# Moving the 16 padding transfers of each FFN from SyncE's queue ahead of the expert tiles to between the loads of tiles 24 to 31, with another order of tiles

## The reference

```
scores = softmax(xt @ Wg.T)                       # 16 experts in 4 groups
# the best 2 groups by their best expert, then the best 4 experts inside them
h = silu(einsum('td,eid->eti', xt, W1)) * einsum('td,eid->eti', xt, W3)   # inner width 176
y = sum over the 4 chosen experts of (h @ W2[e].T) * score
z = silu(xt @ Ws1.T) * (xt @ Ws3.T) @ Ws2.T       # shared expert, inner width 352
x = x + y + z
```

## Time and profile before

| | |
|---|---|
| Three executions, median | 1353.41 us (1342.67 to 1368.69) |
| The profiled execution's own time | 1349.85 us, of which the span of the trace is 1348.1 us |
| TensorE matmuls busy | 1144.7 us, 85% of the span |
| VectorE, ScalarE, GpSimd busy | 873.5, 541.6, 689.1 us |
| Chain that ended last | TensorE 57%, VectorE 18%, issue 6%, DMA 6%, ScalarE 6%, GpSimd 2%, SyncE's queue 2% |
| DMA | 169.84 MB, mean 126 GB/s |
| Padding transfers | 32 issues, 66.2 KB each |

### The profile page before, as it was taken

The page is one execution under the profiler, slowest core; times in us unless marked ns, Lnnn a source line. Parts: engine busy times, 40 slices in busy tenths (PEclk is TensorE's granted clock), DMA queues, the critical chain, the costliest instruction groups (busy, mean ns, idle before and its releaser), DMA issues.

```text
span 1348.1 us, 26055 instructions
## 1 busy us (share of the span) xinstructions
PE 1144.7 (85%) x8706; PEld 614.0 (46%) x8706; DVE 873.5 (65%) x2067; ACT 541.6 (40%) x846; POOL 689.1 (51%) x841
## 2 busy tenths in 40 slices
PE   6888999998899699999288899999779859999990
PEld 2343444342655366566154344444246435665650
DVE  5688899981576145555388899999568523554543
ACT  2124777779431122222032577777844001222210
POOL 4452344544036577767552454545521652787671
PEclk9897999999889799999699899999988978999995
DMA  4424433320825479987754321221062345898868
GB/s 144 144 86 126 122 109 121 106 64 2 287 72 149 150 183 164 158 156 113 192 178 143 108 61 53 62 50 50 3 255 48 113 129 144 168 159 161 153 91 262
DMA packets 145875, 169.84 MB, mean 126 GB/s; under 512 B 20240, under 2 KB 130768, under 8 KB 145232
## 3 DMA queue, kind: packets, MB, share of 16 engines
q1 hardware_dynamic: 115856, 128.79, 32.7%
q0 software_dynamic: 29184, 38.36, 16.7%
q10 hardware_dynamic: 704, 1.02, 0.2%
HBM read 93.29 MB, written 76.18 MB: 126 GB/s over the span
## 4 chain that ended last, share of the span: by engine, by line
PE 57%; DVE 18%; issue 6%; DMA 6%; ACT 6%; POOL 2%; SPq 2%; another core or an unknown queue 1%; POOLq 0%; ACTq 0%; DVEq 0%
PE pair_ps L1996 11%; PE o_ps L1761 9%; ACT arena L849 4%; DVE nm L1123 4%; PE pair_ps L2029 4%; DMA x_slots<-y_sb,slot_i 3%; DVE bm L1123 3%; PE pair_ps L2032 2%; PE t_ps L1787 2%; PE pair_ps L1711 2%; PE pair_ps L1592 2%; PE pair_ps L1691 2%; PE pair_ps L1716 2%; PE pair_ps L2003 2%; PE pair_ps L1686 2%
## 5 line engine op out<-in xcount | busy, mean ns | idle before, releaser
L849 ACT ACTIVATE arena<-pair_ps 128x1024 f32<-128x1024 f32 x320 | 322.9, 1024 | 130.6 <-PE pair_ps L1686 75.9
L625 POOL TENSOR_SCALAR_AFFINE_SELECT arena<-arena 128x512 f32<-128x512 f32 (+1 forms) x320 | 175.0, 547 | 241.4 <-ACT arena L849 240.9
L1123 DVE TENSOR_REDUCE nm<-pair_ps 128x2 f32<-128x1024 f32 (+1 forms) x192 | 232.6, 1222 | 33.4 <-PE pair_ps L1735 29.5
L687 POOL DMA_INDIRECT x_slots<-y_sb,slot_i x128 | 123.6, 966 | 168.0 <-DVE slot_i L1321 94.0
L1761 PE MATMUL o_ps<-arena 128*9 128x512 f32 (+7 forms) x2048 | 176.8, 440 | 4.2 <-POOL arena L625 4.1
L1996 PE MATMUL pair_ps<-arena 128*128 x512 | 168.6, 471 | 2.5 <-ACT arena L900 2.5
L1123 DVE TENSOR_REDUCE bm<-pair_ps 128x8 f32<-128x1024 f32 x128 | 155.3, 1217 | 4.1 <-PE pair_ps L1735 1.0
L703 POOL DMA_INDIRECT y_h<-xnT,dest x80 | 125.3, 1567 | 58.6 <-DVE xnT L1480 31.4
L703 POOL DMA_INDIRECT y_f<-xnT,dest x80 | 124.6, 1558 | 42.0 <-issue 21.2
L1463 DVE TENSOR_TENSOR arena<-arena,pair_ps 128x128 f32<-128x128 f32 x144 | 41.4, 288 | 116.6 <-ACT arena L905 77.1
L1996 PEld LDWEIGHTS pair_ps<-arena 128*128 128x128 f32 x512 | 93.8, 195 | 43.9 <-issue 6.3
(11 more groups left out here) (275 smaller groups left out, 2012.8 us busy)
## 6 DMA issues: line engine op xcount, KB each, us to landing
arena<-x_slots SPq DMA_DIRECT2D x128, 132.5 KB
arena<-in_w SPq DMA_DIRECT2D x4, 2816.0 KB, 18.9
arena<-q_a SPq DMA_DIRECT2D x64, 96.0 KB
arena<-q_b SPq DMA_DIRECT2D x64, 96.0 KB
y_f<-hw SPq DMA_DIRECT2D x11, 512.0 KB, 2.9
y_h<-hw SPq DMA_DIRECT2D x11, 512.0 KB, 2.9
arena<-in_w SPq DMA_DIRECT2D x2, 2048.0 KB, 17.4
arena<-y_f SPq DMA_DIRECT2D x8, 512.0 KB
```

The lines of the kernel that those rows point to most:

```text
L625: pool.affine_select(p, p, pattern, ALU.is_ge, 0.0, base=0, channel_multiplier=-1)\
L687: pool.indirect_dma_start(x_slots, bass.IndirectOffsetOnAxis(ap=slot_i[:, t, k:k + 1], axis=0), y_sb[:, t, :], None).then_inc(sm(f"scat{n ...
L849: act.activation(p_ring[:, U % RING, :], pair_ps[:, pair_at("T", n, u)].rearrange("p a c -> p (a c)"), ACT.Exp, scale=SCALE).then_inc(sm(" ...
L1123: dve.tensor_reduce(dst, src, X, ALU.max, negate=not 2 <= u < 4).then_inc(sm("t_max_done"), 1)
```

## The change

The paddings are no longer issued first. SyncE's queue now starts with the wait for the order of tiles and the stores of x, and it issues two paddings behind each of the loads of tiles 24 to 31 (`PAD_FIRST`, `PADS`). The load of tile 32 waits until all 16 have landed (`PADDED`). For this no tile ahead of 32 may need padding: the tiles are ordered by levels. Level one, as before, are tiles full by the first 10 groups of tokens; level two are the other tiles that are full in the end; then come the rest. So there are two columns where there was one in `full`, in the counts and in the scan, and VectorE's ordering code is written for a list of levels. Mixed tiles stand at 35, 39, ..., 63 instead of 29, 35, ..., 71; the second weights of the first four are loaded at tiles 8, 16, 26 and 34 as before, those of the others at 47, 51, 55 and 59 instead of 41, 47, 53 and 59. The scatters keep their order and number: 52 ahead of the tiles, waits for 40 and for all 64 at the same tiles as before.

```diff
@@ -56,7 +56,7 @@
 NJ = 72
 PLAIN = 64
 MIXED = NJ - PLAIN
-MIX = tuple(range(29, NJ, 6))
+MIX = tuple(range(35, 64, 4))
 MR = 4
 MIX_AT = (8, 16, 26, 34) + tuple(j + 12 for j in MIX[:4])
 ROUND = 1.5 * 2 ** 23
@@ -72,14 +72,15 @@
 
 XR = 8
 WR = 6
-EARLY_T = 10
-EARLY = 24
-LATE_FIRST = 12
+LEVELS = (10, 16)
+NL = len(LEVELS)
+PAD_FIRST, PADS, PADDED = 24, 2, 32
+FIRST_X = 52
 
 assert (ROWS * TOPK + NE * (HALF - 1)) // HALF <= 2 * NJ <= 2 * P and NJ % XR == 0 and XR == 2 * B
 assert ROWS * TOPK // P <= PLAIN and NE <= 2 * MIXED and MIXED == len(MIX) <= XR
-assert all(j % 2 == 1 and j >= EARLY for j in MIX)
-assert EARLY * P <= EARLY_T * P * TOPK - NE * (P - 1)
+assert all(j % 2 == 1 and j >= TOPK * LEVELS[-2] - NE for j in MIX) and MIXED == len(range(MIX[0], MIX[-1] + 1, 4))
+assert PAD_FIRST + NE // PADS <= PADDED <= min(MIX[0], TOPK * NT - NE) and LEVELS[-1] == NT
 SCH = [(0, 128), (128, 128), (256, 96)]
 M_DMAS = 2 * 16
 
...
@@ -215,7 +216,13 @@
-        full = sb("full", [P, 1], BF16)
+        full = sb("full", [P, NL], BF16)
+        lev = sb("lev", [P, NL, NE])
+        lev_r = sb("lev_r", [P, NL])
+        lev_f = sb("lev_f", [P, NL + 2])
+        lev_d = sb("lev_d", [P, NL])
+        lev_v = sb("lev_v", [P, NL + 1])
+        lev_h = sb("lev_h", [P, NL + 1])
...
@@ -492,26 +499,29 @@
             def row_of(j):
                 return sp.value_load(first_row[0:1, j:j + 1], min_val=0, max_val=SLOT_ROWS - P)
 
-            sp.wait_ge(sm("e_pads"), 1 + past(f, 1))
-            for e in range(NE):
+            def padding(e):
                 row = sp.value_load(pad_row[0:1, e:e + 1], min_val=0, max_val=EMPTY - HALF)
                 sp.dma_start(x_slots[ds(row, HALF), :], x_slots[EMPTY:EMPTY + HALF, :]).then_inc(sm("padded"), 16)
+
             sp.wait_ge(sm("e_order"), 1 + past(f, 1))
             for b in range(B - 1):
                 store_x(b)
-            sp.wait_ge(sm("padded"), 16 * NE * (1 + past(f, 1)))
-            for parity in range(2):
-                sp.wait_ge(sm(f"scat{parity}"), 16 * (EARLY_T * TOPK // 2 + past(f, NT * TOPK // 2)))
             for j in range(NJ):
                 if j == 4:
                     store_x(B - 1)
                 if j >= XR:
                     sp.wait_ge(sm("e_x_tr"), j - XR + 1 + past(f, NJ))
                     sp.wait_ge(sm("e_dest"), (j - XR) // 4 + 1 + past(f, NJ // 4))
-                if j == EARLY:
-                    for parity in range(2):
-                        sp.wait_ge(sm(f"scat{parity}"), 16 * (NT * TOPK // 2) * (1 + past(f, 1)))
+                for t, first in zip(LEVELS, (0,) + tuple(TOPK * t - NE for t in LEVELS)):
+                    if j == first:
+                        for parity in range(2):
+                            sp.wait_ge(sm(f"scat{parity}"), 16 * (t * TOPK // 2 + past(f, NT * TOPK // 2)))
+                if j == PADDED:
+                    sp.wait_ge(sm("padded"), 16 * NE * (1 + past(f, 1)))
                 load(j)
+                for e in range(PADS * (j - PAD_FIRST), PADS * (j - PAD_FIRST + 1)):
+                    if 0 <= e < NE:
+                        padding(e)
                 if j in MIX_AT:
                     second_weights(MIX_AT.index(j))
                 if j % 2 == 1:
@@ -718,9 +728,9 @@
             for n in range(TH * TOPK):
                 scatter(n)
             pool.wait_ge(sm("e_slots"), 2 + past(f, 2))
-            for n in range(TH * TOPK, EARLY_T * TOPK + LATE_FIRST):
+            for n in range(TH * TOPK, FIRST_X):
                 scatter(n)
-            late = range(EARLY_T * TOPK + LATE_FIRST, NT * TOPK)
+            late = range(FIRST_X, NT * TOPK)
             for j in range(NJ):
                 result_out(j)
                 for n in late[2 * j:2 * j + 2]:
@@ -1327,10 +1337,10 @@
                 kpre, single, end, pairs, first, last = (tot[:, i, :] for i in range(6))
                 c = spare[:, 0:NE * NE].rearrange("p (i j) -> p i j", i=NE)
                 total = s_ps[:, 0, NT * NE:(NT + 1) * NE]
-                early = s_ps[:, 0, (NT + 1) * NE:(NT + 2) * NE]
+                early = s_ps[:, 0, (NT + 1) * NE:(NT + 1 + NL) * NE].rearrange("p (l e) -> p l e", l=NL)
                 dve.scalar_tensor_tensor(pad_row[:], experts_i, float(REGION), total, ALU.mult, ALU.add)\
                     .then_inc(sm("e_pads"), 1)
-                ch(dve.tensor_scalar(a[:, 0, :], early, 0.5 - HALF, 1.0 / P, ALU.add, ALU.mult))
+                ch(dve.tensor_scalar(lev[:], early, 0.5 - HALF, 1.0 / P, ALU.add, ALU.mult))
                 ch(dve.tensor_scalar(nt[:, 0, :], total, HALF / 2 - 0.5, 1.0 / HALF, ALU.add, ALU.mult))
                 rounded(nt[:, 0, :])
                 ch(dve.tensor_tensor(c, low16.rearrange("p (i j) -> p i j", i=NE),
@@ -1345,15 +1355,18 @@
                 ch(dve.scalar_tensor_tensor(first, kpre, -1.0, nt[:, 1, :], ALU.mult, ALU.add))
                 ch(dve.tensor_scalar(first, first, 0.5, None, ALU.mult))
                 ch(dve.tensor_tensor(last, first, pairs, ALU.add))
-                rounded(a[:, 0, :])
-                ch(dve.tensor_tensor(a[:, 1, :], a[:, 0, :], first, ALU.add))
+                rounded(lev[:])
+                ch(dve.tensor_tensor(lev[:], lev[:], first.unsqueeze(1).to_broadcast([P, NL, NE]), ALU.add))
                 ch(dve.tensor_scalar(a[:, 2, :], last, lane, None, ALU.is_le))
-                ch(dve.tensor_scalar(a[:, 3, :], a[:, 1, :], lane, None, ALU.is_le))
-                ch(dve.tensor_reduce(r[:, 0:2], a[:, 2:4, :], X, ALU.add))
+                ch(dve.tensor_scalar(lev[:], lev[:], lane, None, ALU.is_le))
+                ch(dve.tensor_reduce(r[:, 0:1], a[:, 2, :], X, ALU.add))
+                ch(dve.tensor_reduce(lev_r[:], lev[:], X, ALU.add))
                 ch(dve.tensor_scalar(r[:, 2:3], r[:, 0:1], float(NE - 1), -float(NE), ALU.min, ALU.add))
-                ch(dve.tensor_tensor(r[:, 3:4], r[:, 2:3], r[:, 1:2], ALU.subtract))
-                ch(dve.tensor_scalar(r[:, 3:4], r[:, 3:4], 1.0 + NE, None, ALU.add))
-                dve.tensor_copy(full[:], r[:, 3:4]).then_inc(sm("e_full"), 1)
+                ch(dve.tensor_scalar(r[:, 3:4], r[:, 2:3], 1.0 + NE, None, ALU.add))
+                ch(dve.memset(lev_f[:, 0:1], 1.0))
+                ch(dve.memset(lev_f[:, NL + 1:NL + 2], 0.0))
+                ch(dve.tensor_scalar(lev_f[:, 1:NL + 1], lev_r[:], -1.0, r[:, 3:4], ALU.mult, ALU.add))
+                dve.tensor_copy(full[:], lev_f[:, 1:NL + 1]).then_inc(sm("e_full"), 1)
 
             def pair_units():
 
@@ -1387,11 +1400,13 @@
 
                 r = ordc
                 dve.wait_ge(sm("e_scan"), 1 + past(f, 1))
-                ch(dve.tensor_copy(r[:, 4:5], s_ps[:, 1, 0:1]))
-                ch(dve.tensor_scalar(r[:, 5:6], r[:, 4:5], float(EARLY), lane_late, ALU.min, ALU.subtract))
-                ch(dve.tensor_scalar(r[:, 6:7], r[:, 4:5], float(EARLY), r[:, 3:4], ALU.is_lt, ALU.mult))
-                ch(dve.tensor_tensor(r[:, 7:8], r[:, 4:5], r[:, 5:6], ALU.add))
-                ch(dve.tensor_scalar(r[:, 7:8], r[:, 7:8], r[:, 6:7], r[:, 5:6], ALU.mult, ALU.subtract))
+                ch(dve.tensor_copy(lev_v[:, 0:1], lane))
+                ch(dve.tensor_copy(lev_v[:, 1:NL + 1], s_ps[:, 1, 0:NL]))
+                ch(dve.tensor_tensor(lev_d[:], s_ps[:, 1, NL:2 * NL], lev_v[:, 1:NL + 1], ALU.subtract))
+                ch(dve.tensor_tensor(lev_v[:, 0:NL], lev_v[:, 0:NL], lev_d[:], ALU.add))
+                ch(dve.tensor_tensor(lev_h[:], lev_f[:, 0:NL + 1], lev_f[:, 1:NL + 2], ALU.subtract))
+                ch(dve.tensor_tensor(lev_v[:], lev_v[:], lev_h[:], ALU.mult))
+                ch(dve.tensor_reduce(r[:, 7:8], lev_v[:], X, ALU.add))
                 ch(dve.tensor_tensor(r[:, 7:8], r[:, 7:8], own1[:, 7:8], ALU.add))
                 dve.tensor_scalar(place[:, 0, :], tiles_i, r[:, 7:8], own1[:, 6:7], ALU.is_equal, ALU.mult)\
                     .then_inc(sm("e_place"), 1)
...
@@ -1907,7 +1922,7 @@
                 last = NT if hf == 1 else TH - 1
                 for t in range(last):
                     first = max(t + 1, hf * TH)
-                    n = (TH if hf == 0 else NT + 1) - first + (1 if hf == 1 and t < EARLY_T else 0)
+                    n = (TH if hf == 0 else NT + 1) - first + (sum(t < first_t for first_t in LEVELS) if hf == 1 else 0)
                     mm = pe.matmul(s_ps[:, 0, first * NE:(first + n) * NE].rearrange("p (n e) -> p n e", n=n), ones,
                                    taken[:, t, :].unsqueeze(1).to_broadcast([P, n, NE]), start=False, stop=t == last - 1,
                                    skip_group_check=True)
@@ -1915,7 +1930,8 @@
 
             def scan():
                 pe.wait_ge(sm("e_full"), 1 + past(f, 1))
-                pe.matmul(s_ps[:, 1, 0:1], upper, full[:], start=True, stop=True, skip_group_check=True)\
+                pe.matmul(s_ps[:, 1, 0:NL], upper, full[:], start=True, stop=False, skip_group_check=True)
```

(17 more changed lines are left out.)

## The result

| | kernel before | changed kernel |
|---|---|---|
| device time, median | 1356.72 us of 4 | 1379.77 us of 4 (1378.88 to 1392.61) |
| execution with the trace, own time / span | 1349.85 / 1348.1 us | 1378.88 / 1377.1 us |
| ratio | | 1.023, 95% interval 1.012 to 1.034 |
| once more, on another chip, fast median | 1353.4 of 10 | 1384.0 of 4; ratio 1.020 (1.014 to 1.027) |

The account below looks back on a forecast made before the run. GpSimd's scatters bind the first FFN's opening; the loop looks bound by TensorE, but SyncE's queue hardly waits. Opening -15.2, mixed tiles -2.2, loop +34.6 sum to +17.2 on 1349.85: 1367 us, range 1332 to 1395.

Parts of the forecast that it names:

- the forecast's own range: Whole kernel: 1355 to 1380 us around the forecast, for slower issues or landings, uncovered ordering, start or lead; chance 0.42.
- Paddings into the loop: Expert loops: 16 issues of 1.19 us plus landing, less cover, delay later loads; 16.2 and 18.4 us, +34.6 together.
- landing wait: Load of tile 32 in the expert loop: waits for the last padding to land, 0.85 us per FFN.
- cover: Expert loop: loads' time in hand, 1.9 and 1.4 us, plus a 1.75 us queue pause in the first FFN.
- Paddings out of the opening: Start of each FFN: 0 gained in the first, 17.5 less 2.3 us in the second; -15.2 us.
- freeze: Second FFN's opening: no matmul or VectorE instruction from 1074 to 1085, ScalarE's silu late; taken to belong to the paddings.
- slower start: Second FFN's first tiles: a start following hard on the scatters is slower, giving back 2.3 us.
- the freeze is chance: Rival, opening: freeze comes in some executions with or without paddings, so the -15.2 falls away; 1382 us, chance 0.14.
- Ordering: Opening of each FFN: extra ordering operations, about 1 us, are covered; cost 0 in both.
- Mixed tiles: Tiles 35 to 63: last tile loses its second scatter, 1.85 us less, 0.72 back; -1.1 per FFN, -2.2.
- Hidden: Rival, expert loop: SyncE's queue has more room and the leads absorb 20 us; 1332 us, chance 0.22.
- The freeze moves: Rival, expert loop: paddings stay slow beside GpSimd's transfers, 2.58 us each; 1389 us, in both FFNs 1412; chance 0.22.

Follow-up runs that it names:

- quarter size: Changed kernel with its paddings back in the opening, plus 16 more of 16 rows instead of 64 behind loads of tiles 24 to 31: 1400.1 us, ratio 1.034.
- one per tile: Changed kernel with one padding behind each load of tiles 16 to 31 instead of two behind each of 24 to 31: 1374.9 us, ratio 1.012.
- row numbers read ahead: Changed kernel with the paddings' 16 row numbers read into registers ahead of the wait for the ordering: 1357.0 us, ratio 1.013.
- ScalarE's in both orders: Paddings issued by ScalarE, two behind each silu of chunks 4 to 11: changed kernel 1342.1 us, ratio 0.988; kernel before 1337.0 us, ratio 0.998.

## Why the prediction was right, and where it was not

**Forecast against result.** 1367 was forecast, 1378.9 measured on the execution with the trace: +17.2 against +29.0 (the medians are 23 apart). The mechanism was right, the loop term too small. From first to last transpose the loops are 26.8 and 27.2 us longer, not the 16 to 18 given as a sign of being right. The additions named for the forecast's own range reach 1376, not its stated 1380, so the end of the range held the result with nothing in the sum behind it: that part was luck. The other signs came: TensorE waits for loads at tiles 27, 31 and 35 in both FFNs, and load 32 waits under 1 us.

**Paddings into the loop, +34.6 predicted, +43.8 measured (22.6 and 21.2).** This is the mis-sized term. The landing wait was right (0.85, 0.9 measured) and so nearly was the issue: taken at 1.19 us, while 21.2 without the landing wait leaves 1.27. Some cover was there too. Counted from tile 24 and with the mixed tile allowed for, the load of tile 35, the last for which TensorE waits, is 20.9 and 19.1 us late and its transpose 18.8 and 18.5. So the cover was worth 2.1 and 0.6, where the sum had 3.65 and 1.4; the pause of 1.75 in it stood at load 40, too late to help. What the sum put at nothing is TensorE's time behind its last wait, the largest error: the transpose of tile 36, whose load is there in time, is 22.6 and 21.2 late.

```profile
561.72 0.69 PE L1987 MATMUL o_ps<-c_f,arena 128*128 128x128 f32 x2 [2.57 <-DMA arena<-x_slots]
563.05 0.90 PE L2019 MATMUL pair_ps<-c_f,arena 128*128 128x128 f32 x3 [0.64 <-issue]
563.73 4.88 PE L2012 MATMUL pair_ps<-arena 128*128 x8
```

These 3.8 us (2.7 in the second FFN) are matmuls at the lower clock level (granted 0.50 from 561.72 to 566.00; the eight take 4.88 instead of 2.53) and short idle times between them. Of the 9.2 us by which the term was short, 6.5 are this restart and 2.3 the cover. Behind the earlier gaps the next wait for a load took such a stretch up; behind the last nothing does. The same stretch costs 1.8 to 4.1 us in each of the six loops of the changed kernel's second trace, the quarter size and the one per tile. It and the cover partly cancel, which is why the whole loss looks like SyncE's extra time, in each pair first and second FFN:

| kernel | SyncE longer from load 24 to load 32 | tiles 24 to 37 longer |
|---|---|---|
| changed | 21.2, 19.5 | 22.6, 21.2 |
| changed, once more | 20.8, 20.4 | 21.1, 22.0 |
| quarter size | 20.9, 18.6 | 20.8, 19.2 |
| row numbers read ahead | 12.2, 10.5 | 11.0, 10.6 |
| one per tile (16 to 32; tiles 16 to 37) | 23.3, 21.7 | 21.8, 21.3 |

One for one within 1.7 us, then, but as the sum of a gain and a loss and not because the lead counts for nothing. At tile 38 the lead is back at 10.1 us (9.5 before). The range of the forecast's own case had put 5.1 for a slower issue and nothing for a slow restart. What brings TensorE's clock down was not tested; the traces show it low behind each gap.

**Paddings out of the opening, -15.2 predicted, about -14 measured.** The opening became 19.0 shorter (17.5 forecast) and tiles 0 to 23 of the second FFN 4.9 longer (2.3 forecast). The size is right, for an execution in which the freeze fell into the second FFN; the 4.9 were taken for a slower start, but tiles 0 to 15 vary by more than that for a cause that stays open, so the agreement is partly luck. In fourteen openings without SyncE's paddings (the changed kernel and the one-per-tile version, ScalarE's in both orders) the opening is 67.3 to 72.8 us. In the twelve of the six executions with SyncE's paddings there, eight are between 76.5 and 96.9, at least one in each execution. So the long freezes come with SyncE's paddings, but which opening they fall into is not fixed, and four openings with these paddings had none. The row of reads alone gave 77.5 and 67.1. The rival "the freeze is chance" was right that it varies, and a standstill of 4.56 us came without SyncE's paddings once in the fourteen; an opening over 73 us didn't. How it comes about is not shown.

**Not in the sum:** tiles 0 to 23 of the first FFN, +3.2. Tiles 0 to 15 took from 36 to 50 us over all kernels, the first kernel included (39.0 and 37.1, then 41.6 and 49.2). Its cause stays open.

**Ordering, 0 predicted:** openings of 69.1 and 68.5, against 69.1 and 69.0 with the old order and ScalarE's paddings, show no cost. **Mixed tiles, -1.1 per FFN:** -1.0.

**The rivals.** "Hidden" fell: there was room for 2.1 and 0.6 us, not for 20. By the rule of the Trainium skill, "DMA: Bandwidth & Descriptors", section "Issuing engines are not separate DMA queues", the time to initiate a DMA is usually small beside the DMA; here 16 issues took about 20 us of SyncE's queue per FFN, and the tiles became 21 to 23 us longer. "The freeze moves" fell too: paddings in the loop are 1.27 us each, and among them TensorE stands for loads, not all engines for nothing. The lock named by "Perfetto Trace Analysis", section "DMA Instruction — HWDGE (DVE, Sync)", of the Trainium skill, is not what froze the version that only read row numbers, since SyncE issued no transfer from 1040 to 1092, where its standstill lies.

## What to carry to other kernels

A queue that only issues transfers can be full without any view saying so. Count its time per tile between two issues and compare it with the bound engine's; if it hardly waits, added issues cost nearly their whole duration. Take off the lead at the tightest load behind them, and add what TensorE loses behind its last wait, when it starts again at the lower clock (here 1.8 to 4.1 us); the number of bytes hardly mattered here. Look for an engine with idle time at that place instead: the same 16 transfers cost nothing that could be measured on ScalarE between two silus. Reading an address into a register ahead of a tight stretch took nearly half of such an issue out of it, but reading 16 in a row beside GpSimd's scatters came with a standstill in one opening of two.

## What the runs showed of the hardware

- Reading and checking the 16 row numbers was 9.0 us of SyncE's extra 21.2 and 19.5 in the loop: 12.2 and 10.5 are left without it.
- TensorE, VectorE and ScalarE can stand together beside GpSimd's indirect scatters, for 9.90 us and once for over 10, while GpSimd goes on (6.26 us busy of 9.90). Those over 4.6 us, TensorE's wait for the first loads aside, came only where SyncE had read the paddings' row numbers in a row, with transfers or without; 16 reads and paddings took 22 to 24 us in the three openings without a freeze in which SyncE issued them in a row, and 33 to 44 in the seven with one. A standstill of 4.56 us came while SyncE only waited. What holds the engines, and why tiles 0 to 15 vary by 13 us, was not settled.
- After a gap of 5.55 us TensorE was granted 0.51 of its clock for the next 4.87 us.
